# Keys and values of the 8-head attention made beside the top-32 attention

## The reference, cut to what matters

```python
# block 1: top-32 attention, 4 heads of 32, FiLM and a convolution behind it
scores = einsum('bthd,bghd->bhtg', Q, K) / sqrt(32)
topv, topi = top_k(scores, 32);  probs = softmax(topv)
# block 2: 16-head attention, then a linear layer on fp8-rounded x and weights
x = x + tanh(g_ffn[2]) * (fake_quant_fp8(_layernorm(x)) @ wq.T + bias)
# block 3: 8-head attention, heads of 64, on the same context
k = (context @ Wk).reshape(..., 8, 64);  v = (context @ Wv).reshape(..., 8, 64)
sim = einsum('bihd,bjhd->bhij', q, k) * 64 ** -0.5
out = einsum('bhij,bjhd->bihd', softmax(sim), v).reshape(..., 512) @ Wo + bo
```

## Time and profile before

| | us |
|---|---|
| median of 3 runs | 1424.72 (1424.49 to 1426.15) |
| the profiled execution, its own time | 1425.62 |
| its span | 1423.8 |
| top-32 stage | about 209 to 478 |
| convolution | 478 to 496 |
| FiLM, expert and 16-head stage | 496 to 896 |
| last attention stage | 896 to 1155 |
| mixture of experts | 1155 to 1424 |

### The profile page before, as it was taken

One profiled execution on the slowest core, in us unless ns is written; L12 is line 12 of the kernel. 1 busy time (PEld: TensorE's weight loads), 2 busy tenths in 40 slices (PEclk: granted clock), 3 DMA queues, 4 the chain that ended last, 5 costly groups with the idle time before them and its releaser, 6 DMA issues. The chain is left out here.

```text
span 1423.8 us, 30767 instructions
## 1 busy us (share of the span) xinstructions
PE 1177.9 (83%) x10551; PEld 807.0 (57%) x10551; DVE 995.2 (70%) x3895; ACT 689.7 (48%) x2022; POOL 548.2 (39%) x770
## 2 busy tenths in 40 slices
PE   4768664767766858996899998699999989999998
PEld 3534322434444535663777777266667667776776
DVE  6767568999999269976577877677776644444433
ACT  3344245677775244432345454366666643333343
POOL 4576665677764246534122321334433310000000
PEclk8788785776675779998799999699999999898989
DMA  6400104000001311101000000000000000000000
GB/s 171 99 0 1 46 12 131 16 24 27 27 23 45 115 64 42 38 23 34 3 3 3 3 4 3 1 1 1 1 2 1 2 0 1 15 0 15 0 16 15
DMA packets 61249, 36.62 MB, mean 26 GB/s; under 512 B 19477, under 2 KB 58992, under 8 KB 61106
## 3 DMA queue, kind: packets, MB, share of 16 engines
q1 hardware_dynamic: 59802, 34.48, 8.5%
q10 hardware_dynamic: 1304, 0.33, 0.1%
HBM read 25.21 MB, written 6.42 MB: 22 GB/s over the span
## 5 line engine op out<-in xcount | busy, mean ns | idle before, releaser
L3032 DVE SCALAR_TENSOR_TENSOR k_X<-ps,m_gt,k_X 128x128 f32 (+1 forms) x256 | 72.1, 344 | 120.9 <-PE ps L2916 120.9
L2955 ACT ACTIVATE m_hid<-ps,k_b 128x512 f32<-128x512 f32 x128 | 81.9, 684 | 133.0 <-PE ps L2916 127.6
L2916 PEld LDWEIGHTS ps<-k_w,m_hid 128*128 128x128 f32 x1024 | 123.1, 192 | 26.8 <-issue 19.6
L2905 PE MATMUL ps<-m_xnT,k_w 128*128 128x512 f32 x256 | 128.1, 631 | 1.3 <-PEq L72 1.3
L2916 PE MATMUL ps<-k_w,m_hid 128*128 128x128 f32 x1024 | 123.4, 275 | 0.0
L2576 POOL TENSOR_TENSOR l_p<-l_p,l_rsum 128x512 f32<-128x512 f32 x64 | 65.3, 1041 | 138.0 <-DVE l_rsum L2854 138.0
L2284 DVE TENSOR_REDUCE g_peak<-ps 128x8 f32<-128x1024 f32 x64 | 75.4, 1220 | 43.0 <-PE ps L1973 43.0
L2708 ACT ACTIVATE l_p<-ps,l_shift 128x128 f32<-128x128 f32 x256 | 91.6, 390 | 21.5 <-DVE l_shift L2795 20.3
L1587 DVE MATCH_REPLACE8 v_left<-c_top,v_left 128x128 f32<-128x128 f32 x384 | 100.8, 275 | 0.0
L711 PE MATMUL ps<-f_expT,f_xeT 128*128 128x512 f32 x128 | 77.3, 739 | 27.2 <-DVE k_X L1089 27.2
L2179 ACT ACTIVATE g_pT<-ps 128x1024 f32<-128x1024 f32 x64 | 62.0, 1021 | 71.6 <-PE ps L1989 71.6
(11 more groups left out here) (538 smaller groups left out, 3145.8 us busy)
## 6 DMA issues: line engine op xcount, KB each, us to landing
v_toep<-kpad SPq DMA_DIRECT2D x4, 1024.0 KB, 9.2
fo_dram<-c_fo SPq DMA_DIRECT2D x32, 128.0 KB, 1.7
g_v<-fo_dram SPq DMA_DIRECT2D x8, 512.0 KB, 3.7
d_mine<-d_wad SPq DMA_DIRECT2D x32, 96.5 KB, 1.9
k_X<-in_x SPq DMA_DIRECT2D x8, 256.0 KB, 3.6
v_late<-kpad SPq DMA_DIRECT2D x2, 1024.0 KB, 8.1
out<-k_X SPq DMA_DIRECT2D x8, 256.0 KB, 2.4
f_cx<-in_ctx SPq DMA_DIRECT2D x4, 384.0 KB, 5.4
```

The lines of the kernel that those rows point to most:

```text
L2905: pe.matmul(ps[:, 4 * u + q, :], k.w1_3[:, e, 128 * q:128 * q + 128], xnT[:, u], start=True, stop=True).then_inc(s["hid_ps"].sem, 1)
L2916: m = pe.matmul(ps[:, 4 * u + 2 + e % 2, j * S:j * S + S], hid[:, u, q, j * S:j * S + S], k.w2_3[:, e, q, :], start=q == 0, stop=q == 1)
L2955: act.activation(hid[:, u, q, :], ps[:, 4 * u + q, :], ACT.Gelu, bias=k.b1_3[:, 2 * e + q:2 * e + q + 1]).then_inc(s["hid"].sem, 1)
L3032: dve.scalar_tensor_tensor(out=xj[u][j], in0=ps[:, 4 * u + 2 + e % 2, j * S:j * S + S], scalar=gt[:, u, j, e:e + 1], in1=xj[u][j], op0=ALU ...
```

## The change

**Keys and values.** In turn p of the top-32 stage, `values_keys(2p)` and `values_keys(2p+1)` make the values and keys of the last attention for two batches: for each of the 4 pairs of heads one 128x128 product of values and one of keys, into columns 128:384 of the four banks that hold the scores. ScalarE evacuates each batch in one instruction of 128 x 1024 (`spilled`), and SP stores it to DRAM (`kv_dram`, 512 KB a batch, 16 MB in all). The last stage loads a batch at a time back into three buffers, and has neither the two products nor their evacuations (`kT` on ScalarE, `v` on VectorE).

**fp8 bias.** The add on GpSimd moves from the last stage into the 16-head stage, at step 4g+9 behind the evacuations of the group.

**First queries.** The queries of group 0 are copied out of PSUM by ScalarE, not VectorE.

**Toeplitz chunks.** `EARLY` is 3, not 4: three chunks are loaded early, two into `sc` and `left`, three at the start of the convolution.

```diff
-EARLY = CHUNKS // 2
+EARLY = 3
+            def keep_kv(i):
+                sp.wait_ge(kv_done, i + 1)
+                sp.dma_start(k.kv_dram[:, i, :], kv[:, i % 2].rearrange("p h c -> p (h c)")).then_inc(k.kv_out[i % 2], 16)
...
+                if i % 2 and i + 4 < B:
+                    keep_kv(i + 3)
+                    keep_kv(i + 4)
...
+            def values_keys(i):
+                pe.wait_ge(sc_done, min(i + 2, B))
+                if i:
+                    pe.wait_ge(kv_done, i)
+                c = slice(S * i, S * i + S)
+                for h in range(4):
+                    q = slice(128 * h, 128 * h + 128)
+                    pe.matmul(ps[:, h, 128:256], k.cT[:, c], k.wv3[:, q], start=True, stop=True)
+                    m = pe.matmul(ps[:, h, 256:384], k.wk3[:, q], k.cT[:, c], start=True, stop=True)
+                m.then_inc(kv_ps, 1)
...
+                if pair(p):
+                    values_keys(2 * p)
                 if pair(p + 1):
                     scores(2 * (p + 1))
...
+                if pair(p):
+                    values_keys(2 * p + 1)
                 if pair(p + 1):
                     scores(2 * (p + 1) + 1)
...
+            def spilled(i):
+                act.wait_ge(kv_ps, i + 1)
+                if i >= 2:
+                    act.wait_ge(k.kv_out[i % 2], 16 * (i // 2))
+                act.activation(kv[:, i % 2], ps[:, 0:4, 128:384], ACT.Identity).then_inc(kv_done, 1)
...
+                if (n - 9) % G == 0 and 0 <= (n - 9) // G < GROUPS:
+                    g = (n - 9) // G
+                    pool.wait_ge(o_done, G * (g + 1))
+                    pool.tensor_tensor(group(k.X, g), group(k.X, g), rows(k.bias8), ALU.add)
...
+        @block.sync
+        def _(sp):
+            for i in range(B):
+                if i >= 3:
+                    sp.wait_ge(av_ps, i - 2)
+                sp.dma_start(kv[:, i % 3].rearrange("p h c -> p (h c)"), k.kv_dram[:, i, :]).then_inc(kv_in[i % 3], 16)
...
-                    pool.tensor_tensor(group(g), group(g), rows(k.bias8), ALU.add).then_inc(xb8_done, 1)
...
-                    pe.matmul(ps[:, 6, :], k.wk3[:, 128 * b:128 * b + 128], k.cT[:, W * g:W * g + W], start=True,
-                              stop=True).then_inc(k_ps, 1)
...
-                    pe.matmul(ps[:, 7, :], k.cT[:, S * i:S * i + S], k.wv3[:], start=True, stop=True).then_inc(v_ps, 1)
...
-                    act.activation(kT[:, g % 2, b, :], ps[:, 6, :], ACT.Identity).then_inc(k_done, 1)
...
+                if g == 0:
+                    act.wait_ge(q_ps, b + 1)
+                    act.activation(qT[:, 0, b, :], ps[:, bank(g, b), :], ACT.Identity).then_inc(q_done, 1)
...
-                    dve.tensor_copy(v[:, i % 2], ps[:, 7, :]).then_inc(v_done, 1)
```

More of the change, by code:

```diff
@@ L1187, in stage_film @@
         k.fo_out = [once(f"fo_out{i}") for i in range(2)]
+        k.kv_out = [once(f"kv_out{i}") for i in range(2)]
         k.sc = ctx.enter_context(nc.sbuf_tensor("v_sc", [128, CH, 128], F32))
@@ L1247, in film_in @@
         flip_ps, flipped = once("flip_ps"), once("flipped")
+        kv_ps, kv_done = once("kv_ps"), once("kv_done")
         block = ctx.enter_context(nc.Block())
@@ L1259, in _ @@
                 load_toeplitz(sp, k, c, k.toep[:, c])
+            def keep_kv(i):
+                sp.wait_ge(kv_done, i + 1)
+                sp.dma_start(k.kv_dram[:, i, :], kv[:, i % 2].rearrange("p h c -> p (h c)")).then_inc(k.kv_out[i % 2], 16)
+            for i in range(4):
+                keep_kv(i)
             for i in range(B):
@@ L1496, in _ @@
                 if pair(p):
+                    spilled(2 * p)
+                if pair(p):
                     whole(2 * p + 1)
@@ L1499, in _ @@
                     scored(2 * (p + 1) + 1, p)
+                if pair(p):
+                    spilled(2 * p + 1)
                 if (p + 3) % 2 == 0 and 0 <= (p + 3) // 2 < GROUPS:
@@ L2520, in fp8_attention8 @@
                               "xnT_done"))
-        k_ps, k_done, q_ps, q_done, v_ps, v_done = (
-            once(n) for n in ("k_ps", "k_done", "q_ps", "q_done", "v_ps", "v_done"))
+        q_ps, q_done = once("q_ps"), once("q_done")
+        kv_in = [once(f"kv_in{i}") for i in range(3)]
         sc_ps, top_done, shift_done, p_done, rsum_done, share_done, pT_ps, pT_done, av_ps, oT_done, out_ps, x_done = (
@@ L2626, in _ @@
                     pe.wait_ge(oT_done, i + 1)
-                    pe.wait_ge(v_done, min(i + 2, B))
+                    if i:
+                        pe.wait_ge(x_done, i)
                     pe.wait_ge(x8_done, begun(n - 1, 11))
@@ L2697, in _ @@
                     m.then_inc(o8_ps, 1)
-                b = keys(n)
-                if b is not None:
-                    pe.matmul(ps[:, b, :], k.wk3[:, 128 * b:128 * b + 128], k.cT[:, 0:W], start=True,
-                              stop=True).then_inc(k_ps, 1)
         @block.scalar
@@ L2712, in _ @@
             for n in range(FIRST, LAST):
-                g, b = item(n)
-                if g:
-                    act.wait_ge(k_ps, 4 * g + b + 1)
-                    if g >= 2 and b == 0:
-                        act.wait_ge(sc_ps, G * (g - 1))
-                    act.activation(kT[:, g % 2, b, :], ps[:, 6, :], ACT.Identity).then_inc(k_done, 1)
                 if 0 <= n + 1 < B:
@@ L2754, in _ @@
                                    scale=scale[:]).then_inc(q8_done, 1)
-                b = keys(n - 1)
-                if b is not None:
-                    act.wait_ge(k_ps, b + 1)
-                    act.activation(kT[:, 0, b, :], ps[:, b, :], ACT.Identity).then_inc(k_done, 1)
         @block.vector
@@ L2808, in _ @@
                     dve.tensor_scalar(mag[:], mag[:], E4M3["least"], E4M3["magic"], ALU.max, ALU.mult).then_inc(magic, 1)
-                if 0 <= n + 1 < B:
-                    i = n + 1
-                    dve.wait_ge(v_ps, i + 1)
-                    if i >= 2:
-                        dve.wait_ge(av_ps, i - 1)
-                    dve.tensor_copy(v[:, i % 2], ps[:, 7, :]).then_inc(v_done, 1)
                 g, b = item(n)
-                if g is not None:
+                if g:
                     dve.wait_ge(q_ps, 4 * g + b + 1)
```

48 lines of the change are left out of this document (19 added, 29 removed).

## The result

The changed kernel takes 1465.93 us (1464.08 to 1469.28, 4 runs) beside 1424.63 for the kernel before: a ratio of 1.0284 with a 95% interval of 1.0262 to 1.0307. It is slower by 41 us, outside the range that was forecast (1411 to 1448). Its profiled execution has a span of 1467.5 us, 43.7 above that of before.

A forecast was written before the change was run, and what follows sets the result against it. VectorE was taken to bound the top-32 stage, TensorE being busiest in the last attention stage. Terms +20 +0.5 +0.6 -14.2 gave +6.9 on the profiled 1425.6 us, 1432.5; about 1432 against the median, range 1411 to 1448.

The forecast's parts named there:

- the +20 of the top-32 stage: Top-32 stage: added products and evacuations make turns longer than VectorE's 14.92 us; +20 us, bounds nothing to +55.
- The chain at full clock: Top-32 stage: one turn summed across TensorE and ScalarE, 14.7 us odd, up to 15.5 behind even, mean 15.3.
- In even turns the products of keys and queries come on top, about 0.4 net: Top-32 stage: products of keys and queries lengthen an even turn from 14.7 to 15.1 us.
- The 4.2 us of products behind it ... cost 1.7 more: Top-32 stage: TensorE's clock falls in a 3.9 us gap each turn, so products behind it cost 1.7 us more.
- The ten turns of 17.0 and four of 16.1: Top-32 stage: fourteen turns take 234.4 us against 208.9 at VectorE's 14.92 us, +25.5.
- The 5.5 that I took off: Top-32 stage: deducted from +25.5, 3.8 us of slack used up by first turns and 1.7 where the clock holds.
- the lower clock stays: Top-32 stage rival: mean clock below 0.6, turns over 18 us, +50 to +55, time 1465; chance 0.08.
- VectorE stays the bound: Top-32 stage rival: clock holds, slack absorbs the work, stage gains 0 to 2 us, time 1412; chance 0.30.
- Convolution, +0.5: Convolution: three chunks loaded late instead of two, mostly hidden beside the first products; +0.5 us, between 0 and 3.1.
- 16-head stage, +0.6: 16-head stage: GpSimd's eight moved bias adds hide in waits except the last; +0.6 us, +10 if none hid.
- Last stage, -14.2: Last attention stage: fewer products, no fp8 adds, shorter steps and opening; -14.2 us, bounds -3.5 to -70.
- The floor of 6.29: Last attention stage: shortest step, exponentials to exponentials, 6.29 us, as in old steps without keys and queries.

The follow-up runs named there:

- the keys first: Changed kernel with 14 throwaway products in odd turns' TensorE gap, plus ScalarE evacuating keys and queries ahead of the second full exponentials: 1432.52 us, ratio 1.0043.
- both reorderings: Changed kernel with ScalarE evacuating keys and queries ahead of the second full exponentials, and first scores and spill before the second remainder exponentials: 1412.87 us, ratio 0.9915.

## Why the prediction was wrong

The sign was right and the size was not: +7 forecast, +41 measured. All but 4 us of the miss is one term, the +20 of the top-32 stage, and most of that is one step of its working, the even turns.

- **That the cover is nearly used up and a chain takes over from VectorE**: right. The pairs' distance is 18.7 us, `share` is late, and TensorE waits 3.6 us where 3.9 was forecast.
- **The products added**: the sum counts 16 for each batch. There are eight, recorded as 16. They take 1.88 us a batch at full clock (369.62 to 371.50) where the sum has 2.1, and 3.69 at half, where it has 3.48; the miscount did little harm.
- **The chain at full clock, 14.7 in odd turns and up to 15.5 behind even ones**: right for odd turns, where it could be seen: with 14 throwaway products they take 14.7 to 16.6, and with the keys first too 14.7 to 15.8. No even turn ran at full clock with this order.
- **"In even turns the products of keys and queries come on top, about 0.4 net"**: this is the step that failed. Six even turns took 121.5 us for 100.1 (five of 16.8 and one of 16.1), which is 21 of the 25 us that the fourteen turns missed. The turn shown above, 20.3 for 16.8, has three additions: the second values and keys begin 12.5 us behind its start, not 11.5, as the weight transposes are in part at the lower clock (2.73 us for 2.1) and ScalarE waits 0.77 for the FiLM product, which the products of keys and queries delay; the flip waits 2.14 for `kT`, where the chain has nothing; and scores, values and keys at the lower clock cost 2.0 where 1.7 was counted. I had followed what each added instruction takes, and not what stands behind it on its engine: `kT`'s evacuation stands behind `sc` and the second spill, and another engine waits for it. That order alone is worth 11 us, and 14.5 with the gap of the odd turns filled.
- **"The 4.2 us of products behind it ... cost 1.7 more"**: too small. Behind the gap of an odd turn not only the values and keys run at the lower clock but the scores, transposes and flip too (5.7 us for 3.3, +2.4), and the next weight transposes in part (2.65 for 1.78, +0.9). What it pays to fill that gap is 1.9 us in the odd turn and 1.2 in the even one behind it, 3.1 in all.
- **The ten turns of 17.0 and four of 16.1**: measured 19.1 (251.64 to 442.22) and 17.2 (to 511.07), 259.4 us for 234.4. That is 25 of the 33 us missed here. Before's fourteen took 208.5, so the turns make +50.9 of the +52.7. The 5.5 that I took off, 3.8 of slack and 1.7 for a clock that holds, are not there as such: 4.2 us came on top ahead of the first turn, and 2.4 were given back behind the last.
- **The rival "the lower clock stays"** gave 1465 for a turn of over 18 us, and that is the time measured; but its sign, a mean clock below 0.6, is not there. The mean clock of the stretch from 270 to 440 us rose, from 0.71 to 0.76, as TensorE had more to do, and my own sign of about 0.65 was wrong with it. Its number was right partly by luck, with half of its mechanism: what runs at 0.50 is the part of the turn that is on the path. The mean over a stage doesn't tell that.
- **The rival "VectorE stays the bound"**: its condition was right, that by load all fits (13.8 of 14.92), and its time, 1412, is what the same work takes in another order (1412.87). It fell by the gap, as its counter-argument said, and by the flip's wait, which nothing in it named.
- **Convolution, +0.5**: the mechanism was right, the size too small: 3.4 in the changed kernel, 1.6 with the edit alone.
- **16-head stage, +0.6**: +1.5 measured. The two kernels without the edit take 400.2 and 401.5 in this stage, the ten with it 401.3 to 404.6, so it may cost some us, but neither this term nor a stall of VectorE by the adds is told from nothing. The +10 of the worst case is excluded.
- **Last stage, -14.2**: -13.8. The floor of 6.29 held (6.28), but for two of the last four steps, where the lower clock cost 2.3 us that the sum has no term for. Of the parts, the opening gave 3.7 for 3.0 and the steps 10.0 for 11.2. But "without it 6.63: -3.5" is not the fp8 bias's own: alone it gives 0.8 in the steps, and the rest only once TensorE's products are gone too.
- **The bounds**: the 13.5 us that the rivals and the range take off are not the sum of the terms, which is 13.1 (14.2 - 0.5 - 0.6). It changes no verdict.

## What to carry to other kernels

When work is put beside a bound engine, add up the load first, and then walk the loop: for each added instruction, which instruction stands behind it on its queue, and which engine waits for that one. Here the same added work costs 53 us in one order of ScalarE's queue and nothing that shows in another, that is, with each evacuation placed as soon as its product is ready and ahead of exponentials that nobody waits for yet. A wait that costs nothing while another engine is the bound, as the flip's 1.77 us before, is on the path once the bound has moved. The gaps of TensorE on the path cost twice here, by their length and by the half clock of what followed; with the gap filled by 14 products only its length was paid, and 28, longer than the gap, gave most of that back.

## What was not expected

- 14 throwaway products a turn, in half of the turns, made the kernel 19 us faster (1447.01 for 1465.93).
- Removing a stall from one step lengthened the next by 0.69 of 0.88 us: the late `shift` had hidden a wait for TensorE.
- In some profiles VectorE's MAX8 are recorded as lasting a median of 0.42 us instead of 0.28 (both reorderings, and the run without values and keys, 270 to 440 us), while they start at the same distance (0.19 us) and the pairs take the same time. A busy time made of such records overlaps itself; the distances of starts are what counts.
